# One queue for loads and stores: a subject-mixing kernel issues every transfer from SyncE, each load three transfers behind the store that frees its slot

## The chip, the cores and the metric

The kernel runs on one core of one Trainium2 chip. The time is device microseconds of that core. A profiled execution gives the trace: spans of TensorE (PE, and PEld for its weight loads), VectorE (DVE), ScalarE (ACT), GpSimd (POOL) and SyncE (SP), and the packets of the core's 16 DMA engines with the queue that each came from. In this kernel q1 is the queue of transfers that SyncE issues, and q10 that of ScalarE; q8 and q14 carry instructions.

## The reference

```python
# x: (128, 128, 1024) f32, subjects: (128,) in 0..7, weights: (8, 128, 128) f32
w = weights[subjects]
out = jnp.einsum('bct,bcd->bdt', x, w)
return x + out
```

Each of 128 samples is multiplied by the 128x128 matrix of its subject and added to itself. The input x and the output are 67.1 MB each, the weights 0.5 MB.

## The kernel before

Two samples make a tile of 128 partitions by 2048 f32 (1 MB), 64 tiles in all. The SBUF tensor `ring` holds 16 tiles; 16 tiles are a turn, and there are four turns. Transfers move SPAN = 2 tiles (2 MB) at a time, so the ring has eight slots of two tiles and the whole job is 32 loads and 32 stores. Here S(p) and L(p) mean the store and the load of pair p of tiles, p from 0 to 31; pair p lives in slot p mod 8.

The residual is folded into the weights: the identity is added to each subject's matrix once (`table`), so one product per sample is the whole answer. For each tile POOL copies the two samples' matrices from `table` to `selected`, PE runs 16 matmuls of 512 columns from `ring` into `products` (two PSUM buffers), and then DVE copies the even half and ACT the odd half of the result back into the same slot of `ring`, each in two copies. The output of a pair therefore replaces its input, and the slot is loaded again only when its store is complete.

Everything is ordered by semaphores that the kernel sets by hand. `x_loaded[j]` and `stored[j]` count the transfers of slot j, `even_drained` and `odd_drained` the copies of DVE and ACT.

- SyncE issues the weights (L84), the first eight loads at once (L86), and then in a loop, for each slot in order, waits for `stored` of the slot and issues its next load (L93).
- ScalarE, behind its copies of the second tile of a pair (L208), waits for both engines' copies and issues the store of the pair (L216). At the end it waits for all stores.
- PE waits at the first tile of a pair for `x_loaded` of the slot, and for each tile for `selected` and for a free PSUM buffer.

So loads and stores come from two issuing engines, in two queues, and neither engine's stream holds the other's transfers back except through `stored`.

Of the kernel before, what the change touches and what calls it, by code (L numbers as in the profile page):

```python
# [9 lines left out]
TILES_PER_TURN = 16  # L10

SPAN = 2
PSUM_BUFS = 2
SELECT_BUFS = 4
BANK = 512
DMA = 16
# [4 lines left out]

DRAINED_FREE = 2 * PSUM_BUFS
PRODUCT_FREE = SELECT_BUFS


def subject_mix_kernel(nc: bass.Bass, x: bass.AP, subjects: bass.AP, weights: bass.AP, out: bass.AP):
    samples, channels, times = x.shape
    n_subjects, _, mixed = weights.shape
    row = 2 * times
    tiles = samples // 2  # L30
    turns = tiles // TILES_PER_TURN
# [9 lines left out]
    x_rows = x.rearrange("b (q e) t -> (b q) (e t)", e=2).rearrange("(t p) f -> p t f", p=channels)  # L41
    out_rows = out.rearrange("b (q e) t -> (b q) (e t)", e=2).rearrange("(t p) f -> p t f", p=channels)

    with ExitStack() as ctx:  # L44
        def sem(name):
            return ctx.enter_context(nc.semaphore(name))


        ring = ctx.enter_context(nc.sbuf_tensor("ring", [channels, TILES_PER_TURN, row], F32))
# [9 lines left out]
        subject_row = ctx.enter_context(nc.sbuf_tensor("subject_row", [1, samples], I32))  # L59
        products = ctx.enter_context(nc.psum_tensor("products", [mixed, PSUM_BUFS, 2, times], F32))  # L60

# [11 lines left out]
        weights_selected = sem("weights_selected")  # L73
        x_loaded = [sem(f"x_loaded{s}") for s in range(0, TILES_PER_TURN, SPAN)]
        stored = [sem(f"stored{s}") for s in range(0, TILES_PER_TURN, SPAN)]
        product_ready = sem("product_ready")
        even_drained = sem("even_drained")
        odd_drained = sem("odd_drained")
# [3 lines left out]
        @block.sync  # L82
        def _(sp):
            sp.dma_start(loaded[:], weights.rearrange("n (h l) d -> (n h) (l d)", l=SIDE)).then_inc(weights_loaded, DMA)  # L84
            for s in range(0, TILES_PER_TURN, SPAN):
                sp.dma_start(ring[:, s:s + SPAN], x_rows[:, s:s + SPAN, :]).then_inc(x_loaded[s // SPAN], DMA)  # L86

            with sp.Fori(0, turns - 1) as turn:
                for s in range(0, TILES_PER_TURN, SPAN):
                    tile = turn * TILES_PER_TURN + s  # L90

                    sp.wait_ge(stored[s // SPAN], turn * DMA + DMA)
                    sp.dma_start(ring[:, s:s + SPAN], x_rows[:, bass.ds(tile + TILES_PER_TURN, SPAN), :]  # L93
                                 ).then_inc(x_loaded[s // SPAN], DMA)

        @block.gpsimd
        def _(pool):
# [35 lines left out]
        def _(pe):  # L133
# [17 lines left out]
            with pe.Fori(0, turns) as turn:  # L151
                for s in range(TILES_PER_TURN):
                    tile = turn * TILES_PER_TURN + s
                    k, b = s % SELECT_BUFS, s % PSUM_BUFS
                    if s % SPAN == 0:
                        pe.wait_ge(x_loaded[s // SPAN], turn * DMA + DMA)
                    pe.wait_ge(weights_selected, 2 * tile + 2)

                    pe.wait_ge(even_drained, DRAINED_FREE + 2 * (tile - PSUM_BUFS) + 2)
                    pe.wait_ge(odd_drained, DRAINED_FREE + 2 * (tile - PSUM_BUFS) + 2)  # L160
                    for n in range(banks):
# [11 lines left out]
        def _(dve):  # L173
# [13 lines left out]
            with dve.Fori(0, turns) as turn:  # L187
                for s in range(TILES_PER_TURN):
# [3 lines left out]
                    for b in range(2):  # L192
                        nc.vector.tensor_copy(ring[0:HALF, s, b * times:(b + 1) * times],  # L193
                                              products[b * HALF:(b + 1) * HALF, s % PSUM_BUFS, 0, :]
                                              ).then_inc(even_drained, 1)

        @block.scalar
        def _(act):
            act.dma_start(subject_row[:], subjects.rearrange("(a b) -> a b", a=1)).then_inc(subjects_loaded, DMA)
            act.sem_inc(odd_drained, DRAINED_FREE)  # L200

            with act.Fori(0, turns) as turn:
                for s in range(TILES_PER_TURN):
                    tile = turn * TILES_PER_TURN + s

                    act.wait_ge(product_ready, PRODUCT_FREE + tile + 1)
                    for b in range(2):
                        nc.scalar.copy(ring[HALF:channels, s, b * times:(b + 1) * times],  # L208
                                       products[b * HALF:(b + 1) * HALF, s % PSUM_BUFS, 1, :]
                                       ).then_inc(odd_drained, 1)  # L210
                    if s % SPAN == SPAN - 1:

                        act.wait_ge(odd_drained, DRAINED_FREE + 2 * tile + 2)
                        act.wait_ge(even_drained, DRAINED_FREE + 2 * tile + 2)
                        at = s - SPAN + 1
                        act.dma_start(out_rows[:, bass.ds(tile - SPAN + 1, SPAN), :],  # L216
                                      ring[:, at:s + 1]).then_inc(stored[s // SPAN], DMA)
            for s in range(0, TILES_PER_TURN, SPAN):
                act.wait_ge(stored[s // SPAN], turns * DMA)


# [14 lines left out]
```

## Time and profile before

| what | before |
|---|---|
| median of 3 runs | 324.7 us (324.68 to 325.45) |
| profiled execution: its own time | 324.61 us |
| profiled execution: span of the trace | 322.7 us |
| PE busy | 246.9 us (77%) |
| DVE busy | 160.5 us (50%) |
| ACT busy | 133.8 us (41%) |
| POOL busy | 55.1 us (17%) |
| moved by DMA | 134.80 MB, mean 418 GB/s over the span |
| loads (q1), stores (q10) | 50.1% and 49.1% of the 16 DMA engines' time |

The profiled execution takes 1.9 us more than its span, since launch and end lie outside the trace. Shares are of the span. The two queues' shares are the time of their packets on the 16 DMA engines; added up they say how full these were.

### The profile page before, as it was taken

The numbers are of one execution on the slowest core, as the hardware profiler recorded it, in microseconds if no ns is written. First come the engines' busy times: TensorE is split into PE (matmuls) and PEld (weight loads), VectorE is DVE, ScalarE is ACT, GpSimd is POOL, SyncE is SP. The second block draws the span as 40 slices with busy tenths as digits, with TensorE's granted clock in tenths as the row PEclk, the third lists the DMA queues.
The fourth block names the chain that finished last, engine by engine and source line by source line (L and its number), as shares of the span: only waits on it lengthen the run. The fifth ranks groups of instructions, "written<-read, shape, count | busy, mean of one in ns | idle before, by whom it ended". The sixth has DMA issues, their size and how long they took to land.

```text
span 322.7 us, 3936 instructions
## 1 busy us (share of the span) xinstructions
PE 246.9 (77%) x1088; PEld 119.6 (37%) x1088; DVE 160.5 (50%) x131; ACT 133.8 (41%) x132; POOL 55.1 (17%) x140
## 2 busy tenths in 40 slices
PE   3289999999988786678786888666799686986500
PEld 3244444444444443334333434333344242542200
DVE  0417677677675265653355464446517366363600
ACT  1016466566664243444244443435506244242400
POOL 5032122122121011111111111111102011000000
PEclk9969999999999799999798899999959799798955
DMA  7999999999999999999999999999999999999995
GB/s 285 430 419 420 401 426 430 423 429 430 423 430 429 424 432 427 424 432 427 426 431 428 426 430 428 425 430 429 424 431 429 426 429 429 426 430 428 427 430 216
DMA packets 17559, 134.80 MB, mean 418 GB/s; under 512 B 1041, under 2 KB 1042, under 8 KB 1170
## 3 DMA queue, kind: packets, MB, share of 16 engines
q1 hardware_dynamic: 8848, 67.64, 50.1%
q10 hardware_dynamic: 8706, 67.11, 49.1%
q8 instruction: 2, 0.03, 0.0%
q14 instruction: 3, 0.02, 0.0%
HBM read 67.63 MB, written 67.11 MB: 418 GB/s over the span
## 4 chain that ended last, share of the span: by engine, by line
DMA 42%; PE 41%; issue 5%; DVE 4%; POOL 1%; ACT 1%; DVEq 1%; POOLq 0%; ACTq 0%; SPq 0%
PE products L165 39%; DMA out<-ring 28%; DMA ring<-x 13%; DVE ring L193 3%; PE products L144 2%; ACT ring L208 1%; POOL pick L105 1%; DVEq L44 1%; DVE table L180 1%; POOLq L124 0%; POOL selected L129 0%; ACTq L216 0%; POOL ones L98 0%; DVE pick L176 0%; DVEq L187 0%
## 5 line engine op out<-in xcount | busy, mean ns | idle before, releaser
L165 PE MATMUL products<-ring,selected 64*128 64x512 f32 x1024 | 241.3, 626 | 51.0 <-DVE ring L193 35.3
L193 DVE COPY ring<-products 64x1024 f32<-64x1024 f32 x128 | 156.4, 1222 | 134.6 <-PE products L165 132.7
L208 ACT COPY ring<-products 64x1024 f32<-64x1024 f32 x128 | 128.7, 1005 | 165.0 <-PE products L165 163.4
L165 PEld LDWEIGHTS products<-ring,selected 64*128 64x128 f32 x1024 | 114.9, 198 | 177.0 <-issue 127.7
L129 POOL COPY selected<-table 64x256 f32 x128 | 50.7, 396 | 228.3 <-PE products L165 185.5
L144 PE MATMUL products<-loaded,pick 32*128 32x256 f32 x64 | 5.5, 515 | 4.9 <-DVE pick L176 4.9
L208 ACT ACT_TABLE_LOAD x4 | 5.1, 1283 | 6.0 <-DVE ring L193 2.9
L144 PEld LDWEIGHTS products<-loaded,pick 32*128 32x128 f32 x64 | 4.8, 268 | 5.2 <-POOL pick L105 4.8
L180 DVE TENSOR_TENSOR table<-products,unit 128x1024 f32<-128x1024 f32 x2 | 3.7, 1927 | 5.8 <-PE products L144 5.8
L105 POOL TENSOR_SCALAR_AFFINE_SELECT pick<-ones 32x512 f32<-32x512 f32 x4 | 2.6, 658 | 0.3
L176 DVE COPY pick<-pick 128x512 f32<-128x512 f32 x1 | 0.4, 427 | 4.3 <-POOL pick L105 4.3
L113 POOL TENSOR_SCALAR_AFFINE_SELECT unit<-ones 64x256 f32<-64x256 f32 x2 | 1.1, 529 | 0.1
L98 POOL MEMSET ones<- 128x512 f32 x1 | 0.5, 525 | 0.3 <-POOLq L227 0.3
L227 POOL MEMSET const-float32-0.0<- 128x1 f32 x1 | 0.1, 98 | 0.1
L227 POOL MEMSET const-float32-1.0<- 128x1 f32 x1 | 0.1, 98 | 0.0
L227 POOL MEMSET const-bfloat16-1.0<- 128x1 bf16 x1 | 0.1, 98 | 0.0
L227 POOL MEMSET const-uint8-127<- 128x1 uint8 x1 | 0.1, 97 | 0.0
L227 POOL BASE_LOAD x1 | 0.0, 17 | 0.2 <-issue 0.2
## 6 DMA issues: line engine op xcount, KB each, us to landing
ring<-x SPq DMA_DIRECT2D x32, 2048.0 KB, 21.9
out<-ring ACTq DMA_DIRECT2D x32, 2048.0 KB, 43.8
loaded<-weights SPq DMA_DIRECT2D x1, 512.0 KB, 3.6
subject_row<-subjects ACTq DMA_DIRECT2D x1, 0.5 KB
```

The source lines that it names most:

```text
L44: with ExitStack() as ctx:
L98: nc.gpsimd.memset(ones[:], 1.0).then_inc(ones_ready, 1)
L105: nc.gpsimd.affine_select(pick[part, :, :, 0, :], ones[part, :], [[1, pairs], [-HALF, 2], [-1, HALF]], ALU.is_equal, 0.0, base=0, channel_ ...
L113: nc.gpsimd.affine_select(unit[part, :], ones[part, :wide], [[1, 2], [-1, mixed]], ALU.is_equal, 0.0, base=0, channel_multiplier=2).then_i ...
L129: nc.gpsimd.tensor_copy(selected[part, k:k + 1, :], table[part, bass.ds(subject, 1), :]).then_inc(weights_selected, 1)
L144: last = nc.tensor.matmul(weights_by_pair[:, at:at + wide], pick[part, r, n].rearrange("p g q -> p (g q)"), loaded[part, r * wide:(r + 1) ...
L165: last = nc.tensor.matmul(products[:, b, g, n * BANK:(n + 1) * BANK], selected[part, k, e * mixed:(e + 1) * mixed], ring[part, s, e * time ...
L176: nc.vector.tensor_copy(pick[:, :, :, 1, :], pick[:, :, :, 0, :]).then_inc(pick_doubled, 1)
L180: nc.vector.tensor_tensor(table[:, :, e * mixed:(e + 1) * mixed].rearrange("p n (b m) -> p n m b", b=2), weights_by_pair.rearrange("p (n e ...
L193: nc.vector.tensor_copy(ring[0:HALF, s, b * times:(b + 1) * times], products[b * HALF:(b + 1) * HALF, s % PSUM_BUFS, 0, :]).then_inc(even_ ...
L208: nc.scalar.copy(ring[HALF:channels, s, b * times:(b + 1) * times], products[b * HALF:(b + 1) * HALF, s % PSUM_BUFS, 1, :]).then_inc(odd_d ...
L227: nc = bacc.Bacc("TRN2", target_bir_lowering=False, num_devices=1)
```

## The change

SyncE now issues every transfer. Its stream is written out as pairs: `store(turn, j)` waits until DVE and ACT have copied both tiles of the pair and issues the store; `load(turn, j)` waits until the slot's store is complete and issues the next load into it. Behind S(p) comes L(p+5), the load into the slot of S(p-3), from the fourth store on (LAG = 3); at the end five stores follow the last load. ScalarE issues only the list of subjects, and waits for no transfer. Tiles, buffers, copies and matmuls stay as they are.

```diff
+LAG = 3
...
-            with sp.Fori(0, turns - 1) as turn:
-                for s in range(0, TILES_PER_TURN, SPAN):
-                    tile = turn * TILES_PER_TURN + s
-
-                    sp.wait_ge(stored[s // SPAN], turn * DMA + DMA)
-                    sp.dma_start(ring[:, s:s + SPAN], x_rows[:, bass.ds(tile + TILES_PER_TURN, SPAN), :]
-                                 ).then_inc(x_loaded[s // SPAN], DMA)
+            spans = TILES_PER_TURN // SPAN
+
+            def store(turn, j):
+
+                done = DRAINED_FREE + 2 * (turn * TILES_PER_TURN + SPAN * j + SPAN)
+                sp.wait_ge(even_drained, done)
+                sp.wait_ge(odd_drained, done)
+                sp.dma_start(out_rows[:, bass.ds(turn * TILES_PER_TURN + SPAN * j, SPAN), :],
+                             ring[:, SPAN * j:SPAN * j + SPAN]).then_inc(stored[j], DMA)
+
+            def load(turn, j):
+
+                sp.wait_ge(stored[j], turn * DMA)
+                sp.dma_start(ring[:, SPAN * j:SPAN * j + SPAN],
+                             x_rows[:, bass.ds(turn * TILES_PER_TURN + SPAN * j, SPAN), :]).then_inc(x_loaded[j], DMA)
+
+            for j in range(spans):
+                store(0, j)
+                if j >= LAG:
+                    load(1, j - LAG)
+            with sp.Fori(1, turns - 1) as turn:
+                for j in range(spans):
+                    store(turn, j)
+                    if j >= LAG:
+                        load(turn + 1, j - LAG)
+                    else:
+                        load(turn, j - LAG + spans)
+            for j in range(spans):
+                store(turns - 1, j)
+                if j < LAG:
+                    load(turns - 1, j - LAG + spans)
+            for j in range(spans):
+                sp.wait_ge(stored[j], turns * DMA)
...
-                    if s % SPAN == SPAN - 1:
-
-                        act.wait_ge(odd_drained, DRAINED_FREE + 2 * tile + 2)
-                        act.wait_ge(even_drained, DRAINED_FREE + 2 * tile + 2)
-                        at = s - SPAN + 1
-                        act.dma_start(out_rows[:, bass.ds(tile - SPAN + 1, SPAN), :],
-                                      ring[:, at:s + 1]).then_inc(stored[s // SPAN], DMA)
-            for s in range(0, TILES_PER_TURN, SPAN):
-                act.wait_ge(stored[s // SPAN], turns * DMA)
```

SyncE's stream at the start of the program, before: the weights, the eight first loads, and then the loop, in which each load waits for its own slot's store (`stored0` is slot 0, `stored2` slot 1, since the names count tiles).

```order
L84 DMA loaded<-weights 128x1024
L86 DMA ring<-x 128x2x2048 x8
L88 UNCONDITIONAL_BRANCH
L88 ISA
L93 ISA [waits stored0]
L93 DMA ring<-x 128x2x2048
L93 ISA [waits stored2]
L93 DMA ring<-x 128x2x2048
```

The same place of the changed kernel: behind the eight loads stand S(0) to S(3), and then L(8), S(4), L(9), S(5), L(10).

```order
L86 DMA loaded<-weights 128x1024
L88 DMA ring<-x 128x2x2048 x8
L97 DMA out<-ring 128x2x2048 [waits odd_drained,even_drained] x4
L103 DMA ring<-x 128x2x2048 [waits stored0]
L97 DMA out<-ring 128x2x2048 [waits odd_drained,even_drained]
L103 DMA ring<-x 128x2x2048 [waits stored2]
L97 DMA out<-ring 128x2x2048 [waits odd_drained,even_drained]
L103 DMA ring<-x 128x2x2048 [waits stored4]
```

What moved: four stores stand ahead of the first repeated load, and from there on a load is issued only when the store written ahead of it has been issued.

SyncE's stream at the end of the changed kernel, from the last turn on (there was nothing behind the loop before).

```order
L97 DMA out<-ring 128x2x2048 [waits odd_drained,even_drained]
L103 DMA ring<-x 128x2x2048 [waits stored12]
L97 DMA out<-ring 128x2x2048 [waits odd_drained,even_drained]
L103 DMA ring<-x 128x2x2048 [waits stored14]
L97 DMA out<-ring 128x2x2048 [waits odd_drained,even_drained] x5
L46 UNCONDITIONAL_BRANCH [waits stored8,stored10,stored6,stored12,stored4,stored14,stored2,stored0]
```

These are S(25), L(30), S(26), L(31) and S(27) to S(31), and the wait for all stores, which ScalarE had before.

## Rows read from the trace of the kernel before

**Rows 1.** The page: DMA packets of the whole execution.

```profile
DMA packets 17559, 134.80 MB, mean 418 GB/s; under 512 B 1041, under 2 KB 1042, under 8 KB 1170
```

**Rows 2.** Windows: stretch, length, busy by engine, PE clock, DMA share, GB/s.

```profile
0.00:8.00 8.00, 3.14 (x29) 2.85 (x33) 0.43 (x1) 1.28 (x1) 4.43 (x12) 1.00 0.77 285
8.00:29.00 21.00, 14.43 (x84) 7.61 (x78) 8.38 (x6) 4.02 (x4) 4.75 (x12) 0.84 1.01 423
29.00:32.00 3.00, 3.00 (x16) 1.44 (x14) 2.01 (x3) 1.81 (x2) 0.79 (x2) 1.00 1.01 421
32.00:34.00 2.00, 2.00 (x12) 1.01 (x10) 1.04 (x2) 0.60 (x2) 0.27 (x1) 1.00 0.99 319
34.00:36.00 2.00, 2.00 (x12) 0.88 (x12) 1.97 (x2) 1.61 (x2) 0.52 (x2) 1.00 1.04 438
60.00:290.00 230.00, 188.32 (x802) 90.00 (x800) 122.03 (x101) 104.36 (x103) 38.79 (x98) 0.95 1.01 428
293.00:318.00 25.00, 8.83 (x32) 4.17 (x32) 5.55 (x5) 4.25 (x5) 0.00 (x0) 0.68 1.01 429
318.00:320.00 2.00, 0.00 (x0) 0.00 (x0) 0.00 (x0) 0.00 (x0) 0.00 (x0) 0.50 0.29 123
320.00:322.70 2.70, 0.00 (x0) 0.00 (x0) 0.00 (x0) 0.00 (x0) 0.00 (x0) 0.50 0.04 15
```

**Rows 3.** DMA queues from 60 to 280 us: packets, MB, share of 16 engines.

```profile
q1 hardware_dynamic: 6104, 47.07, 50.6%
q10 hardware_dynamic: 6106, 47.02, 50.5%
```

**Rows 4.** DMA queues from 8 to 18 us, all of them.

```profile
q1 hardware_dynamic: 554, 4.28, 101.2%
```

**Rows 5.** DMA queues from 308 to 318 us, all of them.

```profile
q10 hardware_dynamic: 557, 4.30, 101.6%
```

**Rows 6.** The page: DMA issues, KB each, median us from issue to landing.

```profile
ring<-x SPq DMA_DIRECT2D x32, 2048.0 KB, 21.9
out<-ring ACTq DMA_DIRECT2D x32, 2048.0 KB, 43.8
```

**Rows 7.** SyncE's own waits: us in total, times, longest.

```profile
SPq L93 <- DMA out<-ring: 247.7, 24, 32.5
```

**Rows 8.** The page's groups: ACT's copies, busy, mean ns, idle before.

```profile
L208 ACT COPY ring<-products 64x1024 f32<-64x1024 f32 x128 | 128.7, 1005 | 165.0 <-PE products L165 163.4
```

**Rows 9.** Timeline of ACT: issues of the first four stores and the last.

```profile
29.43 0.43 ACTq L216 DMA_DIRECT2D out<-ring  x1
36.30 0.38 ACTq L216 DMA_DIRECT2D out<-ring  x1
43.16 0.38 ACTq L216 DMA_DIRECT2D out<-ring  x1
50.03 0.38 ACTq L216 DMA_DIRECT2D out<-ring  x1
...
305.46 0.38 ACTq L216 DMA_DIRECT2D out<-ring  x1
```

**Rows 10.** DMA queues from 32 to 34 us: the stores' first packets.

```profile
q10 hardware_dynamic: 17, 0.14, 16.4%
```

**Rows 11.** The repeated loads issued from 260 to 290 us: times, and landing.

```profile
L93 SPq DMA_DIRECT2D ring<-x x2: 372/372/373, 262.1 to 272.1; - x2
...
DMA to landing us min/median/max: 21.5/21.5/21.6
```

**Rows 12.** The chain that ended last, its last piece on PE: start, us, what.

```profile
293.90 8.85 PE products L165 x32
```

**Rows 13.** The eight first loads on SyncE: issue ns min/median/max, first and last start.

```profile
L86 SPq DMA_DIRECT2D ring<-x x8: 424/472/4557, 1.3 to 10.6; - x8
```

**Rows 14.** DMA queues from 18 to 28 us: the two that carry instructions.

```profile
q8 instruction: 1, 0.02, 0.7%
q14 instruction: 1, 0.01, 0.2%
```

## The prediction

> **What bounds it now.** I read the DMA rows first, because the job moves 134.80 MB [rows 1]. The table of stretches gives the rate: from 60 to 290 us the 16 DMA engines are busy all the time (share 1.01) and move 428 GB/s [rows 2]. At that rate the bytes alone take 134.80 / 0.428 = 315.0 us of the span of 322.7 us. So I looked for the other 7.7 us, as length x (1 - rate / 428) of each stretch [rows 2]:
>
> - 0 to 8 us, 285 GB/s: 2.67 us, the start, before and among the first packets.
> - 8 to 32 us, loads alone at 423 and 421: 0.30 us.
> - 32 to 34 us, 319 GB/s: 0.51 us, of which 438 GB/s in the next 2 us gives 0.05 back: 0.46 us. The first packets of the stores' queue fall here: 17 of them, 0.14 MB, by 34 us [rows 10].
> - 318 to 322.7 us, 123 and then 15 GB/s: 1.43 + 2.61 = 4.04 us, the tail, in which a few DMA engines still have packets and the others none. The 15 GB/s of the last 2.7 us are 0.04 MB, which one engine moves in 1.5 us (a sixteenth of 428 is 26.75 GB/s), so the latest engine ends at about 321.5 us, 3.5 us behind the bulk.
>
> Together 7.5 us of the 7.7. Between 36 and 318 us nothing is lost. The reader is to see also that the rate does not depend on what is moved: 428 with both queues half and half [rows 2, 3], 429 from 293 to 318 us [rows 2], where near the end the stores are alone (101.6%, [rows 5]), and the loads alone fill the engines too (101.2%, [rows 4]). No arrangement of full queues can beat the 428 by anything that these rows show.
>
> The compute engines follow. PE has 188.3 us of work in those 230 us [rows 2], and ACT spends 163.4 us waiting for PE's products [rows 8]. SyncE waits 247.7 us for stores [rows 7], which costs nothing while the queues are full.
>
> **The change part by part.** I use one length throughout: a transfer of 2.097 MB at 428 GB/s takes 4.90 us, a pair of load and store 9.80 us.
>
> *ScalarE's issues.* 32 issues of some 0.38 us [rows 9] leave ACT, 12 us in all. ACT waits for PE anyway [rows 8], so I price this at 0.
>
> *SyncE's issues.* SyncE takes over the 32 issues. 0.4 us each, against 4.90 us that the transfer lasts: 0, as long as the queue holds work. It may block for room: one of the first eight loads took 4.56 us to issue [rows 13], since some six transfers fill the queue. A SyncE blocked by a full queue costs nothing either.
>
> *The start.* In the old order the first store joined at about 33 us, while loads 5 to 7 were still in their queue. Now S(0) stands behind all eight loads. Loads with weights are 17.3 MB; by 32 us 2.28 + 8.88 + 1.26 = 12.4 MB have moved [rows 2], and the other 4.9 MB take until 43.4 us. S(0) to S(3) then run until 48.3, 53.2, 58.1 and 63.0. Their data are ready when ACT issued them, at 29.43, 36.30, 43.16 and 50.03 [rows 9], since PE's work of the first turn does not change (every load of it lands earlier than before, not later). The thinnest cover is that of S(3): 58.1 - 50.03 = 8.1 us. From its issue to its first packet the first store took some 3.9 us (issued at 29.43 [rows 9]; 0.14 MB by 34 us at half the rate began at 33.3 [rows 10]). If the cover went, each microsecond missing would be one of idle DMA. I take 0.
>
> The dip of 0.46 us belongs to the moment when the second queue joins. Bounds: it stays (0), or goes (-0.46). With a single queue the nearest row is loads behind loads at a full share [rows 4], so I take -0.46. Loads run alone for 11.4 us longer; at 421 instead of 428 that is up to 0.19 us, of which I take 0.1.
>
> *Steady state.* Behind S(p) comes L(p+5). Between L(p) and S(p) lie eight transfers, 39.2 us. In that time L(p) has to land (the latest engine 3.5 us behind the bulk), and PE and the copies have to finish the pair: the last one took from 293.90 [rows 12] to the issue at 305.46 [rows 9], 11.6 us. Cover: 39.2 - 3.5 - 11.6 = 24.1 us. Between the end of S(p-3) and L(p+5), which waits for it, stand six transfers, 29.4 us. So SyncE's two waits of a pair both end with some five transfers still queued. Behind a waiting store stands only the load after it, and who waits for that is PE, five pairs later. 0.
>
> A page of the Trainium skill speaks against the change: Perfetto Trace Analysis, section DMA Optimizations, advises to give inputs and outputs to different issuing engines, "to allow more dynamic spread", above all with loops. By it a store that is not ready would hold the loads behind it, and the sum would rise; the cover of 24.1 us above says that the trace does not bear it out here.
>
> *Turns of direction inside one queue.* This the trace does not show: no queue holds a store next to a load of the ring. In the new order there are 49 such turns (24 loads between stores, and load 7 to S(0)). Lower bound 0: load behind load and store behind store run at full share [rows 4, 5], and with two queues each engine has packets of both directions side by side, all at 428 GB/s [rows 2, 3]. Upper bound, the nearest row that shows any hitch: the 0.46 us of the first joining, 49 x 0.46 = 22.5 us. The case resembles the first rows more, since there too an engine passes from a packet that reads the one memory to one that reads the other, thousands of times. I take 0.
>
> The same skill, DMA: Bandwidth & Descriptors, section Two DMAs through the same engine are not ordered, says that descriptors of a queue start in order but are pipelined, with separate sides for reading and writing. By it a turn costs nothing and the sum stays; no run so far shows such a turn.
>
> *The tail.* The last load was issued at 272.1 and landed 21.5 us later, at 293.6 [rows 11]. Now five stores follow it, 24.5 us, so with the bulk ending at 318 as before it ends at 293.5 for most engines and by 297.0 for the latest. PE and copies, 11.6 us: S(31) is issued at 308.6. Its turn is at 318 - 4.9 = 313.1. Cover 4.5 us, the thinnest of all, against the 3.9 us from issue to packet above; with the queue already full I expect less than that. 0. The late engines stay late: part of it comes from packets of instructions, which take 0.7% and 0.2% of the 16 engines in 10 us [rows 14], that is 1.1 and 0.3 us of a single engine, and which this change does not spread. I leave the tail as it is.
>
> **Sum.** 324.61 (the profiled execution's own time, span 322.7 and 1.9 around it) - 0.46 + 0.1 = 324.25. The median of the runs lies 0.09 above the profiled one: 324.3 us. Within 0.3% (0.97 us), which is what a measurement here can tell, this is no change.
>
> **The rivals.**
>
> *Turns cost something (slower).* Place: every change of direction in SyncE's queue. It decides from 0.97 / 49 = 0.02 us a turn, so little that the shares of the trace could hide it. For it: the dip at 32 us shows that engines can stumble when another kind of transfer begins. Against: half-and-half traffic at full rate. Price: 1 to 22.5 us; at 0.1 us a turn 4.9 us, 329 us.
>
> *A late store holds the stream (slower).* In the middle this needs a pair that is 24.1 us late, and no wait of PE or ACT comes near. At the end the cover is 4.5 us. 802 matmuls took 188.3 us at a granted clock of 0.95 [rows 2], so the 32 of a pair take 7.1 us at 2.4 GHz and 14.3 at 1.2 GHz, against 8.85 measured [rows 12]. With the last pair wholly at 1.2 GHz S(31) comes 5.4 us later and misses its turn by 0.9 us, or by 4.8 with 3.9 us from issue to packet: 325.2 to 329.1 us. It decides from 1 us of idle DMA. For it: the clock of that stretch was 0.68 [rows 2], with PE idle from the last pair on. This is the page's argument for separate issuing engines, Perfetto Trace Analysis, section DMA Optimizations of the Trainium skill, put into this kernel.
>
> *The tail goes (faster).* If the late engines are late because two queues take turns on them, one queue would end all 16 together. The tail's 0.29 MB (123 x 2 + 15 x 2.7) would take 0.7 us on all engines, until 318.7 instead of 321.5: 2.8 us less, or 1.7 with 1.1 us of instruction packets left on one engine. For it: the tail is the largest loss of all. Against: nothing in the rows ties it to the queues, and the same bytes fall to each engine in both orders. 321.5 to 322.6 us.
>
> **How the numbers follow.** No change 0.68 (own range 323.6 to 325.2: dip kept or gone, loads alone slower or not, 0.3 for the spread of runs and the other way 0.3). Turns cost 0.14. Late store 0.05, counted as slower whole. Tail goes 0.13. That makes faster 0.13, same 0.68, slower 0.19. For the range I leave out most of the tail's case (under 322.4, 0.1) and the dearer half of the two slower ones (over 327.5, 0.1).
>
> **What would show it.** Right: one queue near 100% of 16 engines, 428 GB/s from 60 to 290 us, no dip at 32 to 34 us, SyncE waiting for copies and stores with the DMA share at 1.01 throughout, landing times of stores and loads both about 25 to 34 us (five to seven transfers) instead of 43.8 and 21.9 [rows 6]. A steady rate under 427 would be the turns: 423.8 GB/s for 0.1 us each. A gap in the DMA share near 313 us would be the late store. A bulk that ends at 318 with nothing behind it would be the tail gone. The forecast is wrong if the rate in the middle differs at all, since 1 GB/s there is 0.5 us or more.

## The result and the profile after

The change made the kernel slower: 326.57 us (326.30 to 326.65) against 325.0 (324.68 to 325.45), a ratio of 1.0046 (95% interval 1.0031 to 1.0061). The forecast was no change, 324.3 us; the range given, 322.4 to 327.5, holds the time, the likeliest case's own range, 323.6 to 325.2, does not.

The page of the changed kernel: span, packets, the one queue, and the issues with their median us to landing.

```profile
span 324.5 us, 3863 instructions
...
DMA packets 17559, 134.80 MB, mean 415 GB/s; under 512 B 1041, under 2 KB 1042, under 8 KB 1170
...
q1 hardware_dynamic: 17552, 134.75, 98.7%
...
ring<-x SPq DMA_DIRECT2D x32, 2048.0 KB, 32.5
out<-ring SPq DMA_DIRECT2D x32, 2048.0 KB, 32.0
```

The same bytes in the same number of packets as in [rows 1], all in one queue, and loads and stores now land equally late, some 6.5 transfers behind their issue (compare [rows 6]). Windows of the changed kernel (columns as in [rows 2]) show where the rate falls:

```profile
8.00:18.00 10.00, 3.39 (x42) 2.58 (x36) 3.71 (x2) 0.00 (x0) 1.18 (x3) 0.89 1.01 428
18.00:29.00 11.00, 11.00 (x44) 5.03 (x42) 4.41 (x4) 3.98 (x4) 3.57 (x9) 0.79 1.01 419
32.00:36.00 4.00, 4.00 (x22) 1.98 (x20) 3.01 (x3) 2.48 (x3) 0.79 (x2) 1.00 1.02 424
...
64.00:68.00 4.00, 4.00 (x21) 1.85 (x19) 2.44 (x2) 2.01 (x2) 0.79 (x2) 1.00 1.03 412
68.00:72.00 4.00, 4.00 (x22) 1.98 (x20) 2.81 (x3) 2.38 (x3) 1.03 (x3) 1.00 0.96 389
...
60.00:100.00 40.00, 36.88 (x161) 17.13 (x160) 23.86 (x21) 20.88 (x21) 7.68 (x20) 0.91 1.01 420
...
60.00:290.00 230.00, 185.81 (x777) 87.89 (x776) 120.08 (x99) 102.35 (x101) 38.80 (x98) 0.93 1.01 426
...
100.00:300.00 200.00, 156.15 (x652) 74.29 (x650) 101.11 (x83) 85.49 (x85) 31.12 (x79) 0.94 1.01 428
```

The dip that [rows 2] have from 32 to 34 us is gone from there, and has come back from 64 to 72 us, with the first loads behind the first four stores. There it takes 4 x 16/428 + 4 x 39/428 = 0.51 us, as much as before. From 60 to 100 us as a whole the rate is 420 GB/s, and so from 60 to 290 us 426, where 428 was forecast. From 100 us on one queue moves 428 GB/s like two. By 318 us the changed kernel has moved 0.2 MB less than the kernel before (0.48 instead of 0.29 MB are left). Shared by all 16 engines that would be 0.46 us; the end shows that it was not shared. Windows of 1 us, first of the kernel before:

```profile
319.00:320.00 1.00, 0.00 (x0) 0.00 (x0) 0.00 (x0) 0.00 (x0) 0.00 (x0) 0.50 0.18 74
320.00:321.00 1.00, 0.00 (x0) 0.00 (x0) 0.00 (x0) 0.00 (x0) 0.00 (x0) 0.50 0.06 25
321.00:322.00 1.00, 0.00 (x0) 0.00 (x0) 0.00 (x0) 0.00 (x0) 0.00 (x0) 0.50 0.04 16
322.00:322.70 0.70, 0.00 (x0) 0.00 (x0) 0.00 (x0) 0.00 (x0) 0.00 (x0) 0.50 0.00 0
```

and of the changed kernel:

```profile
319.00:320.00 1.00, 0.00 (x0) 0.00 (x0) 0.00 (x0) 0.00 (x0) 0.00 (x0) 0.50 0.25 106
320.00:321.00 1.00, 0.00 (x0) 0.00 (x0) 0.00 (x0) 0.00 (x0) 0.00 (x0) 0.50 0.25 106
321.00:322.00 1.00, 0.00 (x0) 0.00 (x0) 0.00 (x0) 0.00 (x0) 0.00 (x0) 0.50 0.08 33
322.00:323.00 1.00, 0.00 (x0) 0.00 (x0) 0.00 (x0) 0.00 (x0) 0.00 (x0) 0.50 0.06 25
323.00:324.00 1.00, 0.00 (x0) 0.00 (x0) 0.00 (x0) 0.00 (x0) 0.00 (x0) 0.50 0.04 16
```

Read the last column in units of one DMA engine, 428 / 16 = 26.75 GB/s: before, three engines still work at 319 us and one from 320 to 321.6 (16 / 26.75 = 0.6 of the last microsecond). After the change four work until 321 and one until 323.6. The span grew by 1.8 us and the last engine ends 2.0 us later: that is where the time went. Twelve engines end as before, four end later, and one of them sets the time. The 0.2 MB are, near enough, what those four still had to move.

### The profile page after: what moved, and what is told of

It reads as the page before. It is cut to its first block, busy times and chain, and to the rows that moved or that the text cites. A ratio compares the mean times of both kernels' runs of the same rounds, so it can differ in the third digit from the quotient of the medians.

```text
span 324.5 us, 3863 instructions
## 1 busy us (share of the span) xinstructions
PE 251.5 (77%) x1088; PEld 120.8 (37%) x1088; DVE 160.5 (49%) x131; ACT 133.8 (41%) x132; POOL 55.1 (17%) x140
## 4 chain that ended last, share of the span: by engine, by line
PE 60%; DMA 18%; issue 7%; DVE 6%; POOL 1%; ACT 1%; DVEq 1%; POOLq 0%; SPq 0%
PE products L193 59%; DMA ring<-x 18%; DVE ring L221 5%; PE products L172 2%; ACT ring L236 1%; POOL pick L133 1%; DVEq L46 1%; DVE table L208 1%; POOL selected L157 0%; POOLq L152 0%; SPq L97 0%; POOL ones L126 0%; DVE pick L204 0%; POOLq L157 0%; DVEq L215 0%
## 5 line engine op out<-in xcount | busy, mean ns | idle before, releaser
L193 PE MATMUL products<-ring,selected 64*128 64x512 f32 x1024 | 245.8, 636 | 53.6 <-DVE ring L221 36.1
## 6 DMA issues: line engine op xcount, KB each, us to landing
ring<-x SPq DMA_DIRECT2D x32, 2048.0 KB, 32.5
```

The costliest lines, as they stand in the source:

```text
L193: last = nc.tensor.matmul(products[:, b, g, n * BANK:(n + 1) * BANK], selected[part, k, e * mixed:(e + 1) * mixed], ring[part, s, e * time ...
```

## The experiments

All ratios are to the kernel before, timed beside each run. The first four tell the queue from the order of the transfers, from a blocked SyncE and from where the programs lie.

**Two queues, the order of the change.** ScalarE issues the stores as before; SyncE keeps every wait, and so each load still follows the copies of the pair ahead of it.

```diff
 def store(turn, j):
     done = DRAINED_FREE + 2 * (turn * TILES_PER_TURN + SPAN * j + SPAN)
     sp.wait_ge(even_drained, done)
     sp.wait_ge(odd_drained, done)
-    sp.dma_start(out_rows[...], ring[...]).then_inc(stored[j], DMA)
# ScalarE: the waits and the store of the kernel before, put back
```

> The order and all the waits of the change, but ScalarE issues the stores again, in its own queue; SyncE still waits for the copies of the pair ahead of each load. One-queue theory (a transfer behind another in one queue lets single DMA engines fall further behind, and the latest engine sets the end): the time of the kernel before, 325.0 us. Order theory (the loads come later because each waits for a store's data, whatever the queue): the time of the change, 326.5 us, with the bulk of the packets ending at 318 us and the latest engine near 323.6.

Measured: 325.39 us, 1.0011 (1.0001 to 1.0022). Windows of this run:

```profile
68.00:72.00 4.00, 4.00 (x20) 1.83 (x18) 3.01 (x3) 2.58 (x3) 1.19 (x3) 1.00 1.00 426
...
319.00:320.00 1.00, 0.00 (x0) 0.00 (x0) 0.00 (x0) 0.00 (x0) 0.00 (x0) 0.50 0.16 66
320.00:321.00 1.00, 0.00 (x0) 0.00 (x0) 0.00 (x0) 0.00 (x0) 0.00 (x0) 0.50 0.06 25
...
322.00:323.00 1.00, 0.00 (x0) 0.00 (x0) 0.00 (x0) 0.00 (x0) 0.00 (x0) 0.50 0.06 25
```

The dip at 68 us is gone, and from 320 us on a single engine works. By the times most of the loss belongs to the queue, and some 0.1% of the time to the order and the waits. The profiled execution took 325.8 us, the upper end of its runs, and its one late engine works until some 323 us, over 1 us longer than in the kernel before. So the number of late engines at 320 us is one thing, and the end of the latest, which sets the time, another.

**LAG = 2.**

```diff
-LAG = 3
+LAG = 2
```

> The change with LAG = 2: a load follows the store two transfers ahead of it, so six stores instead of five follow the last load and the queue is less deep (four transfers instead of six between the awaited store and the load). One-queue theory: 326.5 us, as the change. Full-queue theory (SyncE blocked by a full queue from 78 us on hands out its packets unevenly): 325.0 to 325.5 us, and issues of some 0.4 us throughout. Late-last-store theory (S(31), issued at 312.5 us, is too late): 326.1 us at the least, as only some 0.1 to 0.4 us of idle DMA is seen at 313 us.

Measured: 326.11 us, 1.0028 (1.0018 to 1.0038). How long SyncE's issues of stores took (ns min/median/max) in the change from 78 us on, and in this run, with its last store; and a window of this run's end:

```profile
L97 SPq DMA_DIRECT2D out<-ring x24: 372/3954/4871, 77.6 to 299.5; - x24
```

```profile
L97 SPq DMA_DIRECT2D out<-ring x26: 372/1084/4853, 64.5 to 293.9; - x26
...
L97 SPq DMA_DIRECT2D out<-ring x1: 372/372/372, 303.8 to 303.8; - x1
```

```profile
320.00:321.00 1.00, 0.00 (x0) 0.00 (x0) 0.00 (x0) 0.00 (x0) 0.00 (x0) 0.50 0.23 98
```

The typical store is held up by 0.7 us instead of 3.6, the kernel is still slower by 1 us, and four engines are late (98 / 26.75 = 3.7). The full-queue theory, which wanted 325.5 us at most, falls as the main cause; single issues still took up to 4.85 us. The time is the 326.1 us that the late-last-store theory allowed. S(31) is issued at 303.8 us here, nearly nine before the 312.5 of the change, and 1 us of loss is left, so a late last store can be no more than a part.

**SyncE's loops written out**, in the kernel before and in the change: the same transfers, other programs.

```diff
-            with sp.Fori(0, turns - 1) as turn:
+            for turn in range(turns - 1):
```

> The kernel before with SyncE's loop of repeated loads written out, the same transfers in the same order and queues. A control on where the programs lie. One-queue and order theories: 325.0 us, no change. Instruction theory (packets of instructions that fall on the latest engine set the end, and any other program moves them): a change of 0.3 to 1 us in either direction.

Measured: 324.87 us, 0.9991 (0.9981 to 1.0001).

```diff
-            with sp.Fori(1, turns - 1) as turn:
+            for turn in range(1, turns - 1):
```

> The change with SyncE's loop over the two middle turns written out, the same transfers, order and queue. One-queue and order theories: 326.5 us, as the change. Instruction theory: 325.3 to 327.2 us, as the packet of instructions that came at 136 us in the change comes at another time or on another engine.

Measured: 326.35 us, 1.0030 (1.0021 to 1.0040). One window of the first, two of the second:

```profile
320.00:321.00 1.00, 0.00 (x0) 0.00 (x0) 0.00 (x0) 0.00 (x0) 0.00 (x0) 0.50 0.08 33
```

```profile
68.00:72.00 4.00, 4.00 (x20) 1.85 (x18) 3.01 (x3) 2.58 (x3) 1.19 (x3) 1.00 0.97 389
...
320.00:321.00 1.00, 0.00 (x0) 0.00 (x0) 0.00 (x0) 0.00 (x0) 0.00 (x0) 0.50 0.23 98
```

One late engine with two queues, four with one, the dip at 68 us again. Where the programs lie moves the time by 0.1 to 0.2% at most and doesn't explain the loss.

**One queue for half of the kernel.** SyncE waits as in the change throughout, and the stores of two turns go to ScalarE.

```diff
+early, late = gate, store   # gate: the waits alone; store: waits and issues
+for turn in range(turns):
+    for j in range(spans):
+        (early if turn < turns // 2 else late)(turn, j)
...
# ScalarE issues the stores of the other two turns
```

> Same order and waits as the change; ScalarE issues the stores of the first two turns (two queues until some 160 us), SyncE those of the last two (one queue). In the runs so far the lost rate and the growing lag of single engines lie between 60 and 100 us, and from 100 us on one queue and two move 428 GB/s alike. Early-turns theory (only the first turns from stores to loads in one queue cost): 325.3 us, as with two queues, and some 0.25 us or less over the kernel before. Every-turn theory (each of the 49 turns costs a little on the late engines): half of what one queue adds, 325.7 to 326.0 us.

Measured: 325.64 us, 1.0024 (1.0014 to 1.0034). It lies between two queues and one, and the intervals reach from the one to the other. A window of the end:

```profile
320.00:321.00 1.00, 0.00 (x0) 0.00 (x0) 0.00 (x0) 0.00 (x0) 0.00 (x0) 0.50 0.12 49
```

Two engines are late, neither one nor four. The run decides nothing by itself.

> The mirror image: SyncE issues all of the first two turns (one queue until some 160 us), ScalarE the stores of the last two. Early-turns theory: 326.3 us, as the change, with less than 400 GB/s in some stretch between 64 and 72 us. Every-turn theory: 325.7 to 326.0 us, like its mirror image.

Measured: 331.92 us, 1.0221 (1.0201 to 1.0240). A window:

```profile
180.00:200.00 20.00, 8.04 (x32) 3.64 (x30) 4.89 (x4) 4.02 (x4) 1.58 (x4) 0.74 1.01 408
```

With PE busy for 8 of 20 us the pass from one queue to two has made loads late, and the kernel waits for them. Its time says nothing on what it was meant for, and its rate from 64 to 72 us was 414 and 406 GB/s, not under 400.

**Transfers of one tile**, in one queue and in two.

```diff
-SPAN = 2
+SPAN = 1
-LAG = 3
+LAG = 6
```

> The change with transfers of one tile (1 MB, SPAN = 1, LAG = 6, so the same lag in bytes): twice the turns, 97, each after half as many packets. Early-turns theory: it lies about as far above its own two-queue counterpart of one tile (the next run) as the change above the kernel before, 1.2 us (0.8 to 1.6). Every-turn theory: twice as far, 2.4 to 3 us.

Measured: 327.90 us, 1.0092 (1.0077 to 1.0107).

> The kernel before with transfers of one tile: the counterpart of the run above. All theories: the packets are the same 8 KB, so 325 us, within 0.5 us of the kernel before.

Measured: 325.83 us, 1.0034 (1.0020 to 1.0048). A window of the end of each, one queue first:

```profile
320.00:321.00 1.00, 0.00 (x0) 0.00 (x0) 0.00 (x0) 0.00 (x0) 0.00 (x0) 0.50 0.25 107
```

```profile
320.00:321.00 1.00, 0.00 (x0) 0.00 (x0) 0.00 (x0) 0.00 (x0) 0.00 (x0) 0.50 0.12 49
```

One queue costs 327.90 - 325.83 = 2.07 us here, against 1.57 in the change: with twice the turns neither the same nor twice as much. Again four engines are late in one queue. The counterpart itself missed its forecast: it takes 1.06 us more than the kernel before, where 0.5 at most was expected.

**The transfers alone.** Nothing is computed; loads go into four slots and stores come from the other four, always the same data. SyncE issues store, load, store, load (first run), SyncE loads and ScalarE stores (second), SyncE all loads and then all stores (third).

```diff
# one queue, in turn
+for i in range(spans):
+    store(sp, i)
+    if i + 2 * half < spans:
+        load(sp, i + 2 * half)
# two queues: the loads in SyncE's program, in ScalarE's
+for i in range(spans):
+    store(act, i)
# one queue, apart
+for i in range(spans):
+    load(sp, i)
+for i in range(spans):
+    store(sp, i)
```

> The transfers alone: the same 32 loads and 32 stores of 2 MB in one queue, in turn from the first store on, with nothing computed (no weights, no products; the stores write out the first loaded tiles again and again). Measures the disputed cost by itself, beside the next two runs. Queue theory (loads and stores in turn in one queue cost whatever else the core does): 1 us or more above the next run. Compute theory (the loss needs the instructions or the copies of the compute engines): within 0.3 us of the next run. The floor: 134.2 MB at 428 GB/s are 313.6 us, with 2.8 us at the start and 1.9 us around the span some 318.3 us and the tail.

> The same transfers alone with the stores in ScalarE's queue and the loads in SyncE's; nothing computed. All theories: near the floor of 318.3 us plus a tail, under 321 us. If single engines fall behind because of the compute engines' instructions, the tail is under 1.5 us here; if not, some 3 us as in the whole kernel.

> The same transfers alone in one queue, all loads first and then all stores, so with a single turn; nothing computed. Queue theory, if the turns cost: the time of the two queues or less. If one queue costs without turns too: above the two queues, like the first run.

Measured: 324.02 us in turn (323.31 to 324.84), 320.09 in two queues (320.01 to 320.29), 322.58 apart (322.25 to 322.70). Windows (POOL, the only engine listed, is idle; then PE clock, DMA share, GB/s) of the three, in that order:

```profile
100.00:160.00 60.00, 0.00 (x0) 1.00 1.01 423
...
318.00:321.00 3.00, 0.00 (x0) 1.00 0.58 243
```

```profile
100.00:160.00 60.00, 0.00 (x0) 1.00 1.01 428
...
315.00:318.00 3.00, 0.00 (x0) 1.00 0.72 306
318.00:321.00 3.00, 0.00 (x0) 1.00 0.00 0
```

```profile
100.00:160.00 60.00, 0.00 (x0) 1.00 1.01 422
160.00:220.00 60.00, 0.00 (x0) 1.00 1.01 428
...
280.00:300.00 20.00, 0.00 (x0) 1.00 1.01 419
```

The clearest result: with nothing computed one queue in turn is 3.9 us slower than two (1.2%). It moves 423 GB/s where two queues move 428. Apart, with one turn, it is still 2.5 us (322.58 - 320.09): the loads alone, until some 160 us, run at 422, the stores behind them at 428 at first and at 419 from 280 us on, which stays unexplained.

That doesn't mean that most of the loss in turn needs no turns, for the two one-queue runs lose in different packets. The traces keep how long each packet of 8 KB took. In two queues it is 309 ns from 36 to 300 us. With loads alone (20 to 155 us, 6953 packets) nearly all take a little longer, 314 on average, and none 330 or more. In turn (36 to 300 us, 13,628 packets) most take 309, and 241 take 330 or more. What packets took over 309 ns adds up to 3.2 us for each of the 16 engines there, and those 241 make 2.6 of it, or 0.05 us for each of the 49 turns. That they belong to the turns is inferred: 197 of them come while the last transfer to land was a store, and neither the loads alone nor the stores alone from 165 to 255 us have any; but the stores alone from 265 to 310 us have 91 of 2304, without a turn.

The compute theory falls. In two queues all engines end together, before 318 us, and in each of the three runs the 16 engines finish the last transfer within 0.7 us of each other.

**Less work for one engine at the end.**

```diff
+for part in (slice(0, 120), slice(120, 128)):
+    act.dma_start(out_rows[part, ...], ring[part, at:s + 1]).then_inc(stored[s // SPAN], DMA)
```

> The kernel before with its last store cut in two, partitions 0 to 119 and 120 to 127, so that (if a transfer of 120 partitions goes to 15 engines and one of 8 to eight) the sixteenth engine has 16 packets less and eight others two more each. Theory that a single engine sets the end, if it is the sixteenth: 323.5 to 324.2 us (0.9 to 1.5 us less, up to the next-latest engine). If it is another one: 325.0 to 325.7 us, no gain.

Measured: 328.08 us, 1.0101 (1.0081 to 1.0121). One window:

```profile
314.00:318.00 4.00, 0.00 (x0) 0.00 (x0) 0.00 (x0) 0.00 (x0) 0.00 (x0) 0.50 0.94 297
```

The stretch that holds both parts of the split store moves 297 GB/s where the whole one has 428 (which part is slow, the window doesn't tell), so the split costs more than any engine could save, and which engine is the latest stays unknown.

**Engines put out of phase.** Was one queue slow because it cannot keep an engine full, or because all 16 engines load at once? An extra load of 8 or 4 partitions ahead of the others puts some engines behind.

```diff
+sp.dma_start(ring[0:8, 8:16], x_rows[0:8, 8:16, :]).then_inc(weights_loaded, DMA)
 for i in range(2 * half):
+    if i == half:
+        sp.wait_ge(weights_loaded, DMA)
     load(sp, i)
```

> The bare transfers in one queue, in turn, nothing computed, with one more load ahead of them: partitions 0 to 7 of eight tiles, 0.5 MB, which if it goes to eight engines puts these half a transfer (eight packets, 2.45 us) behind the other eight for good. In-phase theory (16 engines that all load, and then all store, at the same time lose 1.3% while loading): 426 to 429 GB/s from 100 to 300 us, instead of 422 to 423, and since the eight engines carry 2.45 us more, about the same end. Queue theory (a single queue cannot keep an engine full while it loads): 422 to 423 GB/s still, and 2 us more.

> The same with partitions 0 to 3: if it goes to four engines, these carry eight packets more, as the four late engines of the whole kernel do in effect. In-phase theory: 424 to 428 GB/s from 100 to 300 us, between the bare run and the one with eight engines. Queue theory: 422 to 423 GB/s.

> The change, with the same extra load of partitions 0 to 7 right behind the weights. In-phase theory: no stretch under 420 GB/s between 64 and 72 us, where the change had 412 and 389; the time between 325 and 327.5 us, as the eight engines end 2.45 us later and it is open whether the latest engine is one of them. Queue theory: the dip between 64 and 72 us stays, and 327 to 329 us.

Measured: 335.45, 329.23 and 335.04 us (1.0314, 1.0134, 1.0309). The start with the extra load took far longer than its bytes (166 GB/s in the first 16 us of the third run), so the times say nothing and the rates are what is left. Windows of the run with 8, with 4, and of the whole kernel with 8:

```profile
100.00:160.00 60.00, 0.00 (x0) 1.00 1.01 410
160.00:220.00 60.00, 0.00 (x0) 1.00 1.01 426
220.00:280.00 60.00, 0.00 (x0) 1.00 1.01 418
```

```profile
100.00:160.00 60.00, 0.00 (x0) 1.00 1.01 428
```

```profile
64.00:68.00 4.00, 4.00 (x22) 1.95 (x20) 3.01 (x3) 2.58 (x3) 1.02 (x3) 1.00 1.00 424
68.00:72.00 4.00, 4.00 (x20) 1.83 (x18) 2.98 (x4) 2.56 (x4) 1.20 (x3) 1.00 1.01 426
```

One queue does reach 428 GB/s, with nothing added but the extra load at the start, after which four engines stay 1.7 to 2.8 us behind the others (second run, also 428 from 160 to 280 us; of its 10,444 packets from 100 to 300 us only 11 take 330 ns or more). That ends the theory that a queue alone cannot keep an engine full. But with 8 engines behind the rate wanders between 410 and 426, worse than with none, against the in-phase theory as I had put it. In the whole kernel the dip is gone. The rate goes with how the engines stand to each other; the rule behind it is open.

## Why the prediction was wrong, step by step

**Bulk: right but for one stretch.** The rate of 428 GB/s as the floor, the compute engines idle beside it, and nothing to gain from ScalarE's issues all held. Loads and stores land after 32.5 and 32.0 us (25 to 34 was forecast). But the prediction named the rate from 60 to 290 us as its own sign, and that is 426, because of the 420 from 60 to 100 us.

**"I leave the tail as it is": the step that failed.** The forecast took the late engines for a constant of the kernel (4.04 us of loss from 318 us on). In every run of the whole kernel with one queue throughout (the change, LAG = 2, loop written out, one tile) some four engines still work between 320 and 321 us (106, 98, 98 and 107 GB/s), in every one with two queues one or two (25, 25, 33, 49). (Left out are the runs with the split store and with the extra load.) The end moved from 321.6 to 323.6 us, the whole of the loss. The rival on the tail had the right place and the wrong sign: it let one queue end all engines together.

The semaphores show when the four fell behind. A transfer raises its semaphore 16 times, which I read as once for each engine, and the traces keep these times. For the last store of the kernel before, the last four of the 16 come 1.3, 1.5, 1.7 and 3.6 us behind the first; of the changed kernel 2.6, 2.7, 3.2 and 5.4, with the other twelve within 0.6 us in both. In the changed kernel they are 0.5, 0.8, 1.1 and 1.8 us behind at S(1), 54 us, and 2.4, 2.8, 2.9 and 3.4 at S(7), 103 us. So the low rate from 60 to 100 us did not delay all engines alike but set four of them back, and no rate after 100 us brings that back. The latest engine has more to it: it goes on falling behind in both kernels, by 1.6 us between 152 and 289 us before (at the stores) and by 1.8 us between 147 and 294 us after. That drift is a large part of the old tail; it is there with two queues and with one, and its cause is open. Packets of instructions delay it too (0.7 us at 136 us), but both kernels have five of them, so these don't make the difference.

**"I take 0" for the turns: the second step, mis-sized.** The rows on which the 0 rested were loads alone from 8 to 18 us (101.2%, [rows 4]) and stores alone at the end, without a turn. In the bare transfers a turn costs up to 0.05 us, if all long packets are due to turns, above the 0.02 from which the rival was to decide. The rival had the right sign and 329 us for its time, at 0.1 us a turn dearer than the 326.57 measured. In the whole kernel the price falls due only in the first turns: of the changed kernel's packets of 8 KB, 46 of 2159 take 330 ns or more from 58 to 100 us, and 14 of 10,440 from 100 to 300 us, once four engines stand apart. That the one brings about the other fits the bare run with four engines set apart (428 GB/s), but no run switches the turns off with all else the same. The rival's sign was also mis-summed: a pair of transfers holds two turns, so that 0.1 us each would be 428 x 9.8 / 10.0 = 419 GB/s, not 423.8.

The prediction took 0.1 us for loads that run alone for 11.4 us longer. The size of their rate was right: the bare run has 422 GB/s for loads alone, with no packet of instructions in any queue.

**Dip gone (-0.46 us): wrong.** It moved, to where loads first follow stores.

**The advice against the change** (the Trainium skill, Perfetto Trace Analysis, section DMA Optimizations: inputs and outputs from different issuing engines) was set aside because no store would hold a load back. That part of the working held: SyncE's waits left hardly a gap in the DMA share (0.96 from 68 to 72 us is the lowest of the windows behind the start and before the end). The runs agree with the advice all the same, by 1.0046 against 1.0011 with the stores back in ScalarE's queue, and not by the held loads that I, and not the page, had tied to it.

**Late last store: nearly.** Three reads of the changed kernel: the last load's issue and landing, its pair on PE in the chain that ended last, and the last store's issue with the window around it.

```profile
L103 SPq DMA_DIRECT2D ring<-x x1: 4626/4626/4626, 266.9 to 266.9; - x1
...
DMA to landing us min/median/max: 32.5/32.5/32.5
```

```profile
299.77 10.16 PE products L193 x32
```

```profile
L97 SPq DMA_DIRECT2D out<-ring x1: 373/373/373, 312.5 to 312.5; - x1
```

```profile
313.00:318.00 5.00, 0.00 (x0) 0.00 (x0) 0.00 (x0) 0.00 (x0) 0.00 (x0) 0.50 1.00 416
```

The load landed at 299.4, not 297.0, since the latest engine was later, PE took 10.16 us instead of 8.85, and the store was issued at 312.5 instead of 308.6: of 4.5 us of cover 0.6 were left. It was enough but for 5 x 12/428 = 0.14 us of idle DMA. The 3.9 us from issue to first packet did not recur.

## What to carry to other kernels

When the DMA engines are full, look at the end engine by engine: a last column in units of one engine's rate shows how many are late, and the latest sets the time. Loads and stores in two queues were worth 0.35 to 0.5% here (without and with the change of order) and 1.2% for the transfers alone, even though the same 16 engines carry both: in turn in one queue they ran at 423 GB/s, in two queues at 428. A loss need not be shared: 0.2 MB would have cost 16 engines 0.46 us, and cost four of them 1 to 2 us each. And a price of 0 needs a row that shows the thing priced: stretches of loads alone and of stores alone say nothing on turns between them.

## What was not expected of the hardware

- The bare transfers take 320.09 us in two queues and 324.02 in one.
- One queue with loads and stores in turn runs at 423 GB/s with its engines together, at 428 with four of them apart, and at 410 to 426 with eight apart.
- Loads alone have packets of 314 ns on average, loads and stores in two queues 309.
- Splitting one store of 128 partitions into 120 and 8 brought the rate at the end from 428 to 297 GB/s.
- Where something is computed, single engines end 1.3 to 5.4 us late; with the transfers alone only those do that an extra load had set apart. Packets of instructions are a part of that (1.1 and 0.3 us near 20 us, [rows 14]), and so is one engine that falls behind by some 0.06 us in each transfer of 4.9 us; why it does stays open.
